# Softmax attention in two layers of a one-core network: probabilities left unnormalised, values with a ones column as moving operand, one normalisation per batch, new engine orders

## What is computed

```python
# layer 2, _L2_xattn_ref
content = jnp.einsum('bthd,bThd->bhtT', q + r_w_bias, k)
pe = _sinusoid_reversed(b, kv_t, DMODEL) @ Wp + bp
rel = jnp.einsum('bthd,bThd->bhtT', q + r_r_bias, pe)
rel = _relative_shift(rel)       # pad one column, reshape, drop the first row
attn = (content + rel) * (1.0 / math.sqrt(HEAD_DIM))
attn = attn * mask - 10000000000.0 * (1.0 - mask)
p = jax.nn.softmax(attn, axis=-1)
out = jnp.einsum('bhtT,bThd->bthd', p, v).reshape(b, t, DMODEL)
return out @ Wo + bo
# layer 3, _L3_xattn_ref: the same without rel and mask
scores = jnp.einsum('bhqd,bhkd->bhqk', q, k) / np.sqrt(HEAD_DIM)
attn = jax.nn.softmax(scores, axis=-1)
out = jnp.einsum('bhqk,bhkd->bhqd', attn, v)
return out @ Wo + bo
```

## Time and profile before

| | us |
|---|---|
| median of 3 runs | 2166.54 (2166.14 to 2167.79) |
| the profiled execution: its span | 2165.0 |
| layer 2 attention, from 1150.7 to 1560 | 409 |
| layer 3 attention, from 1657 to 1930 | 273 |
| DVE busy in the two stages | 294 and 188 |
| PE busy in the two stages | 265 and 191 |

### The profile page before, as it was taken

The page is one execution under the profiler, slowest core; times in us unless marked ns, Lnnn a source line. Parts: engine busy times, 40 slices in busy tenths (PEclk is TensorE's granted clock), DMA queues, the critical chain, the costliest instruction groups (busy, mean ns, idle before and its releaser), DMA issues. The chain is left out here.

```text
span 2165.0 us, 32942 instructions
## 1 busy us (share of the span) xinstructions
PE 1479.0 (68%) x9593; PEld 1171.9 (54%) x9593; DVE 1407.6 (65%) x3515; ACT 633.9 (29%) x2082; POOL 339.8 (16%) x472
## 2 busy tenths in 40 slices
PE   4769999999999760000234667667497777659998
PEld 2348888888888650000013445445286555538887
DVE  5866666666666476947574877877543777765555
ACT  2322121212121130000001655555343555443332
POOL 4740000000000010000011322322210010122221
PEclk9669999999999855555555666666598788869999
DMA  5530000000000141041622232232122111000000
GB/s 179 182 91 6 10 5 6 9 5 10 5 10 6 49 121 25 0 78 20 179 78 80 103 139 103 104 136 99 62 65 62 33 31 34 27 16 18 19 19 18
DMA packets 109582, 121.13 MB, mean 56 GB/s; under 512 B 13506, under 2 KB 101395, under 8 KB 105044
## 3 DMA queue, kind: packets, MB, share of 16 engines
q1 hardware_dynamic: 92048, 102.70, 15.4%
q10 hardware_dynamic: 17476, 17.75, 2.9%
HBM read 84.62 MB, written 35.80 MB: 56 GB/s over the span
## 5 line engine op out<-in xcount | busy, mean ns | idle before, releaser
L1770 PE MATMUL L_r_ps<-ident,L_prob 128*128 128x128 f32 x512 | 114.7, 382 | 138.6 <-ACT L_rel L1665 52.6
L698 DVE TENSOR_TENSOR moa_oe<-moa_y_ps,moa_ogT 128x1024 fp32r<-128x1024 f32 x128 | 155.3, 1223 | 76.6 <-PE moa_y_ps L765 74.8
L1770 PEld LDWEIGHTS L_r_ps<-ident,L_prob 128*128 128x128 f32 x512 | 81.3, 193 | 177.4 <-ACT L_rel L1665 63.4
L91 PE MATMUL moa_k_ps<-moa_w_out_hi,moa_oe 128*128 128x256 f32 x512 | 155.6, 304 | 11.9 <-DVE moa_oe L698 11.9
L1138 PE MATMUL warp_t_ps<-ident,warp_entry 128*128 128x128 f32 x1 | 0.5, 473 | 221.6 <-DVE warpb_hit L1121 221.6
L93 PE MATMUL moa_k_ps<-moa_w_out_hi,moa_oe 128*128 128x256 f32 x512 | 143.8, 281 | 0.0
L92 PE MATMUL moa_k_ps<-moa_w_out_lo,moa_oe 128*128 128x256 f32 x512 | 143.6, 280 | 0.0
L1644 ACT ACTIVATE L_xnT<-L_a_ps 128x256 f32<-128x256 f32 x32 | 12.3, 384 | 428.7 <-PE L_a_ps L1712 428.7
L1449 POOL TENSOR_TENSOR L_att<-L_masked,L_mask_add 128x512 f32<-128x512 f32 x64 | 86.7, 1364 | 227.3 <-DVE L_masked L1546 227.3
L1138 PEld LDWEIGHTS warp_t_ps<-ident,warp_entry 128*128 128x128 f32 x1 | 0.2, 183 | 221.9 <-DVE warpb_hit L1121 221.9
L91 PEld LDWEIGHTS moa_k_ps<-moa_w_out_hi,moa_oe 128*128 128x128 f32 x512 | 96.9, 189 | 24.7 <-issue 14.8
(11 more groups left out here) (323 smaller groups left out, 4159.4 us busy)
## 6 DMA issues: line engine op xcount, KB each, us to landing
bounce<-L_rel SPq DMA_DIRECT2D x16, 1032.0 KB, 3.9
L_shifted<-bounce SPq DMA_DIRECT2D x16, 1024.0 KB, 4.8
ret_staged_values<-in_w_value_dram ACTq DMA_DIRECT2D x8, 512.0 KB, 3.8
ret_staged_outputs<-in_w_out_dram ACTq DMA_DIRECT2D x8, 512.0 KB, 3.9
ret_cT<-in_ctxT_pairs_dram SPq DMA_DIRECT2D x16, 256.0 KB, 2.9
L_x<-x_after SPq DMA_DIRECT2D x32, 128.0 KB, 2.1
L_cT<-in_ctxT_pairs_dram SPq DMA_DIRECT2D x32, 128.0 KB, 2.1
L_res<-x_after SPq DMA_DIRECT2D x32, 128.0 KB, 2.1
```

Of the source, the lines that this page charges most:

```text
L91: pe.matmul(out, x_hi, w_hi, start=first, stop=False)
L698: dve.tensor_tensor(oe[e % 2][:, :, :, :].rearrange("p a m s -> p a (m s)"), y_ps[e % 2][:, :, :].rearrange("p m s -> p (m s)").unsqueeze( ...
L1770: last = pe.transpose(r_ps[g % 2][:, j, :], prob[:, 4 * g + j, :], k.ident[:, :])
```

## The change

- The exponentials are no longer summed by ACT (`accum_out` is gone) and no longer multiplied by the inverse sums. `v` gets a 17th column of ones for each head, so that the value product gives the sum beside the 16 outputs. Sums are inverted and outputs normalised once a batch (`over_sums`: one reciprocal of 128 x 16, one product of 128 x 256).
- In the value product the transposed probabilities of one head are now the stationary operand (128 columns) and that head's `v` is the moving one, 17 columns: sixteen products a batch in place of eight. Its result is not transposed; two transposes on PE (`transpose_outputs`) and one copy on ACT (`copy_outputs`) follow the normalisation, in place of `o_even` and the odd heads' addition.
- The scale 1/sqrt(16) goes into the queries and their biases; the scaled mask and the scaled maxima are gone.
- `rel` and `shifted` have the positions innermost. They are written and read in four DMAs of four heads each, in runs of 516 and 512 bytes.
- The output projection writes to the queries' bank `a_ps`.
- PE, ACT and DVE have new orders, apart for the two layers; POOL does the inverse root between the mask additions.

The core of the diff:

```diff
-                        last = act.activation(prob[:, h, :], source(h), ACT.Exp, bias=bias[:, h:h + 1], scale=scale,
-                                              accum_out=total[:, h:h + 1])
+                        last = act.activation(prob[:, h, :], source(h), ACT.Exp, bias=nmax[:, h:h + 1])
...
+                def over_sums(n):
+
+                    dve.wait_ge(pv_done, after(n + 1))
+                    dve.reciprocal(rtotal[:, :], heads_out[:, :, HD]).then_inc(rt_ready, 1)
...
+                    dve.tensor_tensor(o_norm[:, :].rearrange("p (h d) -> p h d", d=HD), heads_out[:, :, 0:HD],
+                                      rtotal[:, :].unsqueeze(2).to_broadcast([128, H, HD]), ALU.mult).then_inc(norm_ready, 1)
...
+                def project_values(n, v_):
+                    pe.wait_ge(norm_ready, after(n - 1))
...
+                def weigh_values(b, u, g):
+                    if g == 0:
+                        pe.wait_ge(norm_ready, after(b))
+                        pe.wait_ge(oT_ready, after(b))
+                    pe.wait_ge(pT_ready if g % 2 else pT_ready_act, after(b * 2 + (g // 2 + 1)))
+                    for j, h in enumerate(heads_of_bank(g)):
+                        last = pe.matmul(b_ps[:, h * VD:h * VD + VD], pT[:, 4 * g + j, :], v[:, u, h, :], start=True, stop=True)
...
+                def step_relative(b, u, ahead=True, front=True, middle=True, tail=True):
...
+                    if tail:
+                        transpose_outputs(b - 1)
+                        pe.wait_ge(oT_ready, after(b))
+                    if front:
+                        project_values(b + 1, nu)
+                        scores(b + 1)
...
+                def transpose_x(n):
+                    pe.wait_ge(ln.xn_ready, after(n + 1))
+                    pe.wait_ge(k_ready, after(n))
+                    pe.wait_ge(xo_ready, after(n - 2))
```

More of the change, by code:

```diff
@@ new lines, in step_relative @@
+                    if front:
+                        copy_queries(b + 1)
+                        for r in range(4):
+                            relative_out(r)
+                    if tail:
+                        copy_outputs(b - 1)
+                    if middle:
+                        exponentials(b, 0, lambda h: att[:, h, :])
+                        exponentials(b, 1, lambda h: att[:, h, :])
+                        copy_transposed(b, 0)
+                        exponentials(b, 2, lambda h: att[:, h, :])
@@ L1683, in step @@
                     if ahead:
                         copy_x(b + 2)
[L1685 to L1690 removed]
+                    if middle:
+                        exponentials(b, 3, lambda h: att[:, h, :])
+                        copy_transposed(b, 2)
@@ new lines, in queries_and_keys @@
+                def queries_and_keys(n, v_):
+                    pe.wait_ge(cT_loaded[v_], loads(n, v_))
+                    pe.wait_ge(xT_ready, after(n + 1))
+                    for off, wt, src in ((0, wq, xnT), (D, wk, cT[v_])):
+                        for m in range(DT):
+                            for t in range(DT):
+                                last = pe.matmul(a_ps[:, off + m * S:off + m * S + S], wt[:, t, 128 * m:128 * m + 128],
+                                                 src[:, t, :], start=(t == 0), stop=(t == DT - 1))
+                    last.then_inc(qk_done, 1)
@@ new lines, in project_outputs, with relative_scores @@
+                def project_outputs(n):
+                    pe.wait_ge(oT_ready, after(n + 1))
+                    for t in range(DT):
+                        last = pe.matmul(a_ps[:, D:2 * D], oT[:, t, :], wo[:, t, :], start=(t == 0), stop=(t == DT - 1))
+                    last.then_inc(out_done, 1)
+                def relative_scores(n, r):
+                    rows = slice(32 * r, 32 * r + 32)
+                    for half in range(2):
+                        last = pe.matmul(r_ps[r % 2][:, 2 * half:2 * half + 2, :], qrT[rows, half, :],
+                                         pz[rows, half, :, :], start=True, stop=True, tile_position=(32 * r, 0))
+                    last.then_inc(rel_done, 1)
@@ new lines, in scores @@
+                def scores(n):
+                    pe.wait_ge(k_ready, after(n + 1))
+                    pe.wait_ge(q_ready, after(n + 1))
+                    for r in range(4):
+                        pe.wait_ge(att_ready if relative else prob_ready, after(n * 4 + (r - 3)))
+                        rows = slice(32 * r, 32 * r + 32)
+                        for half in range(2):
+                            last = pe.matmul(s_ps[r][:, 2 * half:2 * half + 2, :], qT[rows, half, :], kz[rows, half, :, :],
+                                             start=True, stop=True, tile_position=(32 * r, 0))
+                        last.then_inc(s_done, 1)
```

482 lines of the change are left out of this document (239 added, 243 removed).

## The result

| | before | after |
|---|---|---|
| median of 4 runs, us | 2166.34 | 2217.1 (2212.97 to 2221.25) |
| ratio to before, 95% interval | | 1.023 (1.0213 to 1.0247) |
| span of the profiled execution | 2165.0 | 2219.5 |
| a step of layer 2, and its mean clock | 23.3, 0.65 | 27.3, 0.63 |
| a step of layer 3, and its mean clock | 15.8, 0.84 | 16.3, 0.81 |

The changed kernel is 2.3% slower, 50.8 us by the medians and 54.5 between the two profiled executions. The prediction was 2222, 55 more.

The account below looks back on a forecast made before the run. No engine fills a stage; the step is a chain from engine to engine, with the clock deciding. Layer 2 +52, its last two steps -3, layer 3 +6, together +55 on the 2166.5 median: 2222 us, range 2140 to 2285.

Parts of the forecast that it names:

- +52, -3, +6: Forecast us: layer 2 over 14 steps, layer 2's last two steps, layer 3 over 14 steps; together +55.
- 13.05 + 8.35 / clock: Layer 2's new step in us, both legs summed: 21.4 at full clock, 29.75 at half, 27.0 at the assumed 0.60.
- Leg A: Layer 2, end of DVE's last pT copy to first maxima: 10.7 us at full clock, 16.45 at half.
- leg B: Layer 2, first maxima to DVE's last pT copy: 10.7 us at full clock, 13.3 at half.
- the copy of x is a new wait: Layer 2, ACT: copy of transposed x holds up last four exponentials, pT copy and next step's front; the copy takes 0.4.
- So 3.0 + 1.8 us: Serial work said to enter layer 2's first leg, with the value projection behind ACT's output copy, behind all relative copies.
- The value product: PE: 32 instructions in place of 16, started 0.213 us apart at half clock, 0.112 at full; 6.8 or 3.6 a batch.
- Three groups lie beside exponentials in part; the last one stands open: Value product on PE, groups of four heads, each 1.7 us at half clock or 0.9 at full; last group not hidden.
- Layer 3: Step of 6.25 + 7.5 / clock, PE's chain closing on itself; 16.25 us at the assumed 0.75, +0.45 a step.
- Rival A: Clock stays full: layer 2's step 21.4 us (-1.9), layer 3's 13.75 (-2.05), total 2108; chance 0.20.
- Rival C: Removed normalisation products lay wholly on the path and nothing new is: 96.3 us less, 2070; chance 0.04.
- Rival D: Short DMA runs bring `shifted` too late: 1.9 us in 14 steps, +28 on top, 2250; chance 0.03.

Follow-up runs that it names:

- e6: Changed kernel with ten unread products a step added on PE in layer 2, where PE waited; 2180.39 us, ratio 1.0065.
- e1: Changed kernel, layer 2 alone: PE makes the value projection right behind queries and keys, ahead of the relative scores; 2149.96 us, ratio 0.9936.
- e2: Changed kernel, layer 2 alone: ACT copies the transposed x behind the last exponentials and the copy of pT; 2165.34 us, ratio 0.9992.
- e4: Changed kernel, both layers: value product takes two heads with one weight, 8 calls in place of 16, result altered; 2138.07 us, ratio 0.9861.
- e3: Changed kernel with both layer 2 orders of e1 and e2 together; 2126.64 us, ratio 0.9826.
- e8: e3 with DVE's inverse sums and normalised outputs moved between the second and third addition of shifted scores; 2106.19 us, ratio 0.9716.
- e5: Kernel before, each normalisation product of the probabilities done on 4 of 512 columns, so outputs are not normalised; 2116.04 us, ratio 0.9771.
- e11: e8 with three unread full-size products on PE between layer 2's pairs of relative scores, and a wait ahead of these scores; 2098.1 us, ratio 0.9688.

## Why the prediction was right, point by point

**The total.** By the times of `xo`, the 54.5 us between the profiled executions are: first result of layer 2 11.8 later, 13 steps +51.9, the last two -14.6; from there to the first result of layer 3 +2.9; 13 steps +7.0, the last two -3.6; the rest -0.9. The prediction had +52, -3, +6. The start and the last two steps of layer 2 taken together give -2.8. That this meets the -3 of the sum is partly luck, since the two parts are four and five times as large.

**Layer 2's step.** 27.3 measured, 27.0 forecast. With the clock that came, 0.63, the line 13.05 + 8.35 / clock gives only 26.3. The terms are not to blame, the one mean clock is. Leg A measured 16.60 where the sum at half clock has 16.45, and leg B measured 10.91 at 0.81 where its sum (8.1 + 2.6 / clock) gives 11.3. Together they give 27.75 for 27.5 in this step. The line lost 1.4 us against these sums by spreading the full stretch evenly over a step in which it lay in leg B, where it is worth least. That 0.60 was taken instead of 0.63 gave 0.7 of it back, by luck. In e6 the two leg sums at their own clocks give 23.6, which is what was measured. Exponentials 0.30 apart instead of 0.26 do not show: leg B came out below its sum.

**The reason given for it.** That serial work enters leg A by the place of the value projection is borne out by e1, and "the copy of x is a new wait" by e2, whose takings are 3.9 and 3.4 us, clock included. The two sizes in "So 3.0 + 1.8 us" are worked out nowhere in the prediction, and no run separates them. In the trace of after the first shows as 93.0 us that DVE waits in 13 steps for the value projection, the second as up to 1.6 a step that PE waits for exponentials:

```profile
DVE L_v L1503 <- PE L_b_ps L1735: 93.0, 13, 7.4
...
PE L_r_ps L1771 <- ACT L_prob L1638: 34.9, 37, 1.6
PE L_r_ps L1753 <- ACT L_qT L1657: 17.9, 13, 1.4
PE L_r_ps L1753 <- ACT L_rel L1670: 10.5, 13, 0.8
PE L_b_ps L1735 <- ACT L_oT L1644: 6.5, 13, 0.6
```

(us in all, times, longest.)

**The value product.** In the kernel after its instructions start 0.213 us apart at half clock and 0.112 at full, by the median of each; exactly these were taken from eight-column products. An instruction with 128 weight columns and few moving ones thus takes nearly twice as long at half clock, as the prediction held against the rule of the Trainium skill, "TensorE: Matmul & The Clock Gate", section "LDWEIGHTS (loading the stationary operand)". "Three groups lie beside exponentials in part; the last one stands open" is left open by e4, in which more than half of the removed instructions' time was on the path, and perhaps all of it.

**Layer 3.** 16.3 measured, 16.25 forecast, but at a clock of 0.81 for 0.75, where the line gives 15.5. Here too the one mean clock is what fails, not the wait for `xo` ahead of the transpose of x: for that the sum has 1.85 us (DVE's copy, maxima and result), and PE waits 13.8 / 13 = 1.06. On PE, from one such wait to the next, and the stretch of half clock in between:

```profile
1845.04 0.41 PE L1719 MATMUL L_a_ps<-ident,L_ln_xn 128*128 128x128 f32 x2 [1.06 <-DVE L_xo L1519]
1845.29 3.10 PE L1780 MATMUL L_b_ps<-L_v,L_pT 128*128 128x17 f32 x16
...
1861.69 0.41 PE L1719 MATMUL L_a_ps<-ident,L_ln_xn 128*128 128x128 f32 x2 [1.07 <-DVE L_xo L1519]
...
1845.70:1852.50 6.80, 6.80 (x33) 0.50 0.20 58
```

Half clock fell on the last two value groups and on queries and keys, where PE has no wait at all. With the prediction's half-clock terms for these (3.4 and 3.75) and its full-clock terms for the rest (9.9) the sum is 17.05, for 16.65 measured. That a clock of 0.75 in the line came out at 16.25 is therefore luck in part.

**Rival A.** It gave one point from which it decides, 0.79, for a kernel whose orders stay. By the prediction's own lines that is layer 3's; layer 2's is 8.35 / (23.3 - 13.05), 0.81. e6 brought that kernel's layer 2 to 0.81 and its step to 23.6, the step of before being 23.3. So the point for layer 2 is about right, with ten more products in the step; layer 3 missed its own, with 16.3 for 15.8 at 0.81. What A did not see is that orders and clock go together: with PE's waits gone the clock went to 0.81 by itself (e3, e8).

**Rival C.** It priced the removed products at 96; e5 measured 50. The prediction counted 3 us of gain by them in the last two steps and otherwise only the new step's length, and that was right as a sum, but it nowhere said what they were worth: 1.1 and 2.3 us a step.

**Rival D.** No wait for `shifted` in the changed kernel, whose four reads land in 4.5 us. It is right that it sleeps in the slack: in e3's long steps DVE did wait 0.6 us.

**The range.** Its low end, 2140, is called half of A's way from 2150, but half the way to 2108 is 2129; nothing hangs on it here.

**POOL and the transfers' issue** are seen in no wait of after that anybody on the path stands behind.

## What to carry to other kernels

When a change takes work off one engine and gives another more instructions, write down each leg of the step as a + b / clock, before and after, each with its own clock: one mean for the whole step hides where the full stretch falls. The change may be even in work and still lose because the wide products now fall where the clock is low. Look at the order on the engine that becomes the bound, since here three moved lines turned 2.3% slower into 2.8% faster with the same arithmetic. An instruction that has to empty a shared bank should stand on its engine right behind what it waits for, not behind work that nobody waits for.

## What was not expected of the hardware

- Products that nobody reads can shorten a step: ten of 128 x 128 x 512 in bf16 a step gave 37 us in the changed kernel (2217.1 to 2180.39, clock 0.63 to 0.81). Three of them in e11 came out 14 us under three of one row and one weight column at the same place (2098.1, 2112.16, clocks 0.88 and 0.83).
- The mean clock of a stage can stay (0.65, 0.63) while the full stretch moves from one leg of the step to the other (0.82 and 0.51 before, 0.52 and 0.81 after), with the step 4 us longer.
- Steps of a loop with the same instructions differ much with where the clock changes fall: 17.8 and 22.3 to 23.6 us by turns in e3, and 16.1 to 21.8 in e8.
- An exponential of 128 x 128 without a sum starts 0.25 us after the one before in layer 3, with its input in PSUM, and 0.30 in layer 2, with its input in SBUF. With a sum the medians were 0.34 and 0.39.
- 64 reads of 256 KB in runs of 512 bytes, four issued in a row, land in a median of 4.5 us; the 16 reads of 1 MB in 8 KB runs took 4.8 before.
